# Writing out the last 26 instruction loops of an attention and expert layer

## The reference

```python
x = L0_attn_hidden_states                      # (1, 1024, 512)
xn = _layernorm(x, axis=-1)
x = x + _L0_attn_ref(xn, ...) + _L0_ffn_ref(xn, ...)

# attention: 32 heads, latent queries (rank 192) and keys/values (rank 64)
q_lat = rmsnorm(hidden_states @ q_a_w, q_a_norm_w)
q = (q_lat @ q_b_w)...                         # nope 128 + rope 64
ckv = hidden_states @ kv_a_w
scores = (q_nope . k_nope + q_pe . k_pe) * QKD ** (-0.5)
# indexer: 16 heads choose 128 keys for each query
iq = (hidden_states @ idx_wq_w)...; ik = hidden_states @ idx_wk_w
idx_scores = einsum(iw, relu(iq @ ik)) * IDX_D ** (-0.5)
_, topk_idx = jax.lax.top_k(where(causal, idx_scores, -inf), 128)
attn = softmax(where(topk_mask & causal, scores, -inf))
out = (attn @ v) @ o_w

# experts: 8 of rank 16, two for each row
w = gates of the top 2 of softmax(flat @ router_w.T + router_b)
out = einsum('ner,eor->no', (flat @ A) * w, Bm) * SCALING
```

## Time and profile before

| | us |
|---|---|
| median of 3 runs (lowest, highest) | 998.99 (997.48, 999.64) |
| profiled execution, its own time | 999.31 |
| its span, first to last instruction | 997.5 |
| busy: TensorE / VectorE / ScalarE / GpSimd | 895.8 / 740.7 / 680.4 / 449.0 |
| mean granted TensorE clock, share of full | 0.959 |

### The profile page before, as it was taken

How to read it: one execution, slowest core, us unless ns; L and a number is a source line. 1 busy time by engine, 2 the same in 40 slices (tenths; PEclk the granted TensorE clock), 3 DMA queues, 4 the chain that set the end, 5 groups by cost and what they waited for, 6 DMA issues and landing times.

```text
span 997.5 us, 23426 instructions
## 1 busy us (share of the span) xinstructions
PE 895.8 (90%) x7912; PEld 552.9 (55%) x7912; DVE 740.7 (74%) x1593; ACT 680.4 (68%) x1512; POOL 449.0 (45%) x307
## 2 busy tenths in 40 slices
PE   5979999977774689999999999999999999999998
PEld 2434554434441146666676666676766666675443
DVE  5386689999999968777887877787788778783000
ACT  3565779987873367887888788788778878872000
POOL 2194229875656643634554364446335544600000
PEclk9999999997767689999999999999999999999999
DMA  7012111112342920000000000000000000310211
GB/s 228 22 32 63 45 51 54 53 37 75 92 140 100 331 112 2 23 23 24 1 23 23 2 23 23 22 2 23 23 23 3 23 23 1 136 58 22 64 42 42
DMA packets 47261, 52.54 MB, mean 53 GB/s; under 512 B 5440, under 2 KB 31424, under 8 KB 47168
## 3 DMA queue, kind: packets, MB, share of 16 engines
q1 hardware_dynamic: 47168, 51.31, 15.8%
HBM read 36.62 MB, written 6.29 MB: 43 GB/s over the span
## 4 chain that ended last, share of the span: by engine, by line
PE 53%; issue 5%; DVE 4%; ACT 3%; DVEq 0%
PE psS L575 17%; PE psT L652 11%; PE psO L633 8%; PE psS L684 8%; ACT arena L714 2%; DVE arena L1202 2%; PE psT L560 2%; DVE arena L968 2%; PE psT L556 2%; PE psT L558 1%; PE psT L559 1%; PE psT L557 1%; PE psT L641 1%; PE psS L689 1%; ACT arena L914 0%
## 5 line engine op out<-in xcount | busy, mean ns | idle before, releaser
L714 ACT ACTIVATE arena<-psT 128x512 f16<-128x512 f32 (+5 forms) x544 | 262.9, 519 | 121.7 <-PE psT L652 79.3
L968 DVE SCALAR_TENSOR_TENSOR arena<-psT,arena 128x512 f16<-128x512 f32 (+3 forms) x392 | 205.6, 552 | 71.4 <-ACT arena L714 71.4
L575 PE MATMUL psS<-keyT,arena 128*128 128x512 f16 (+3 forms) x1152 | 230.6, 327 | 12.6 <-issue 11.7
L1202 DVE CUSTOM_DVE_ANT_0 arena<-psS,bias 128x1024 f32<-128x1024 f32 (+7 forms) x256 | 192.5, 752 | 53.5 <-PE psS L575 50.9
L914 ACT ACTIVATE arena<-arena,small 128x1024 f32<-128x1024 f32 (+7 forms) x256 | 199.1, 778 | 18.0 <-DVE small L1202 15.9
L652 PE MATMUL psT<-ident,arena 128*128 128x128 f32 x1152 | 176.9, 281 | 9.8 <-DVE arena L968 8.1
L633 PEld LDWEIGHTS psO<-val,arena 128*128 128x128 f16 x3456 | 132.1, 98 | 37.5 <-DVE arena L968 6.0
L575 PEld LDWEIGHTS psS<-keyT,arena 128*128 128x128 f16 x1152 | 103.8, 99 | 84.3 <-issue 30.9
L633 PE MATMUL psO<-val,arena 128*128 128x64 f16 x3456 | 142.7, 193 | 1.2 <-DVE arena L968 1.2
L652 PEld LDWEIGHTS psT<-ident,arena 128*128 128x128 f32 x1152 | 124.3, 142 | 13.3 <-issue 12.9
L1401 POOL TENSOR_TENSOR arena<-arena,cq 128x1024 f32<-128x1024 f32 x16 | 37.8, 2364 | 190.3 <-issue 181.2
(11 more groups left out here) (146 smaller groups left out, 1117.9 us busy)
## 6 DMA issues: line engine op xcount, KB each, us to landing
arena<-in_wiq SPq DMA_DIRECT2D x32, 256.0 KB, 2.8
arena<-in_ow SPq DMA_DIRECT2D x16, 512.0 KB, 4.9
arena<-arena SPq DMA_DIRECT2D x32, 256.0 KB, 2.4
arena<-in_qbT SPq DMA_DIRECT2D x16, 256.0 KB, 2.5
wvo_parts<-arena SPq DMA_DIRECT2D x16, 256.0 KB, 4.6
arena<-in_qpe SPq DMA_DIRECT2D x16, 128.0 KB, 2.8
arena<-in_x SPq DMA_DIRECT2D x8, 256.0 KB, 2.8
out<-arena SPq DMA_DIRECT2D x8, 256.0 KB, 2.0
```

The lines of the kernel that those rows point to most:

```text
L575: last = mm(psS[k % 2][:, c:c + w], Q[:, v, a, h, t * P:(t + 1) * P], keyT[:, b, h, c:c + w], start=(a, b) == (0, 0), stop=(a, b) == (1, 0))
L714: return nc.scalar.activation(dst, src, ACT.Copy, scale=scale)
L968: return v.scalar_tensor_tensor(out=dst, in0=src, scalar=scale, in1=hi, op0=ALU.mult, op1=ALU.subtract)
L1202: v.tensor_tensor_reduce(out=pr[:, k % 4, 0:kw], in0=psS[k % 2][:, 0:kw], in1=bias[:, TOFF[t]:TOFF[t + 1]], scale=-c_s, scalar=3e38, op0=A ...
```

## The change

All 26 loops are written out: each `with engine.Fori(a, b) as i:` becomes `for i in range(a, b):`, which the program that builds the kernel runs itself. The body is emitted once for every value of i with constants in the place of registers. Nothing else differs. One of each kind:

```diff
@@ SyncE, third stage
-            with sp.Fori(1, NP // 2) as i:
+            for i in range(1, NP // 2):
                 load_qw(2 * i, 0, False)
                 load_qw(2 * i + 1, 1, False)
@@ SyncE, value-output products
-            with sp.Fori(1, NP // OW_DEEP) as i:
+            for i in range(1, NP // OW_DEEP):
                 for u in range(OW_DEEP):
                     load_ow(OW_DEEP * i + u, u, False)
                     store_vo(OW_DEEP * i + (u - OW_DEEP), u)
@@ TensorE, projections, and the last stage
-            with pe.Fori(1, NT // 2 - 1) as i:
+            for i in range(1, NT // 2 - 1):
-            with pe.Fori(1, NT // 2) as i:
+            for i in range(1, NT // 2):
@@ ScalarE, third stage
-            with act.Fori(1, IH // 2) as i:
+            for i in range(1, IH // 2):
@@ VectorE, third and fourth stage
-            with dve.Fori(1, IH // 2) as i:
+            for i in range(1, IH // 2):
                 for u in range(2):
                     third(2 * i + u, u, False)
-            with dve.Fori(4, IH // 2) as i:
+            for i in range(4, IH // 2):
                 for u in range(2):
                     fourth(2 * i + u, u, False)
@@ GpSimd, third stage
-            with pool.Fori(1, IH // 2) as i:
+            for i in range(1, IH // 2):
                 for u in range(2):
                     third_sums(2 * i + u, False)
```

More of the change, by code:

```diff
@@ L518, in _ @@
             iq_head(IH, 0, 0, False)
-            with pe.Fori(0, IH // 2 - 1) as i:
+            for i in range(0, IH // 2 - 1):
                 for u in range(2):
@@ L751, in _ @@
             squares(0, True)
-            with act.Fori(1, NT // 2 - 1) as i:
+            for i in range(1, NT // 2 - 1):
                 for u in range(2):
@@ L842, in _ @@
             second_relu(1, 1, False)
-            with act.Fori(1, IH // 2 - 2) as i:
+            for i in range(1, IH // 2 - 2):
                 for u in range(2):
@@ L1131, in _ @@
             second(1, 1, False)
-            with dve.Fori(1, IH // 2 - 1) as i:
+            for i in range(1, IH // 2 - 1):
                 for u in range(2):
@@ L1277, in _ @@
             final(1, 1, True)
-            with dve.Fori(1, NT // 2) as i:
+            for i in range(1, NT // 2):
                 final(2 * i, 0, False)
@@ L1352, in _ @@
             gated_rows()
-            with pool.Fori(3, IH // 2 + 1) as i:
+            for i in range(3, IH // 2 + 1):
                 wq_parts(2 * i, 0)
@@ L1374, in _ @@
             second_sums(1, False)
-            with pool.Fori(1, IH // 2 - 2) as i:
+            for i in range(1, IH // 2 - 2):
                 for u in range(2):
@@ L1435, in _ @@
             rope_low(0, 0)
-            with pool.Fori(1, NP // OW_DEEP) as i:
+            for i in range(1, NP // OW_DEEP):
                 for u in range(OW_DEEP):
```

20 lines of the change are left out of this document (10 added, 10 removed).

## The result

| | before | after |
|---|---|---|
| median of 20 runs (lowest, highest), us | 998.60 (997.45, 1000.43) | 1000.74 (997.61, 1005.52) |
| profiled execution, its own time | 999.31 | 999.08 |
| its span | 997.5 | 997.1 |

A forecast was written before the change was run, and what follows sets the result against it. TensorE was taken to bound the first score and last stages, VectorE's top-128 search the stretch between 142 and 354 us. Terms -0.16, -0.2, -0.6 and -0.2 sum to -1.16 us: 998.99 to 997.8 us, range 994.0 to 1000.8.

The forecast's parts named there:

- Projection loop: Projections, 22 to 37 us: TensorE's idle time at the loop entry goes, -0.16 us.
- Latent products: GpSimd products before the first score loop: a VectorE shift may save or cost 0.95 us; taken as 0.
- Second and fourth stage: VectorE's top-k rounds: written-out and looped rounds already equal, 4.97 and 2.96 us, so 0.
- Third stage (a): Third score stage: fourteen loop rounds each 0.02 us longer than written-out ones; taken as -0.2 us.
- Third stage (b): Third score stage: GpSimd starting 0.2 to 0.4 us sooner shortens two collisions with VectorE, -0.6 us.
- new collisions: Rival, third stage: earlier GpSimd additions hold VectorE's small operations in five rounds, 1002.8 us; chance 0.12.
- Value-output products: Beside the fourth stage: SyncE issues loads and stores sooner, head pairs start earlier, -0.2 us.
- Head pairs: Sixteen head pairs, 354 to 905 us: already written out and untouched by the diff, 0.
- Last stage: Final stage: TensorE is full and the last handover to VectorE already short, 0.
- Instruction fetch: Rival: TensorE's longer program fetches five or six more code blocks, 1 us each, 1003.8 us; chance 0.04.
- branches: Rival: taken loop branches stall VectorE by at most 0.1 us in 17 rounds, removal gives 996.1 us; chance 0.02.
- Slower: Outcome for the whole kernel: measured time above 1001.0 us; chance 0.10, against 0.37 faster and 0.53 the same.

The follow-up runs named there:

- experiment 4: Against before: only ScalarE's and GpSimd's third-stage loops written out, 998.37 us; the whole change except the five third-stage loops, 998.87 us.
- only_third: Before with only the five loops of the third stage written out; 1000.46 us, ratio 1.0021.
- all_again: The whole change, unaltered, run and profiled once more against before; 999.97 us, ratio 1.0011.
- all_apart: Whole change plus the filler, VectorE's first two third-stage low parts reading PSUM instead of SBUF (results not the reference's); 998.15 us, ratio to before 0.9991.
- all_filled: The whole change plus the filler alone; 999.66 us, ratio to before 1.0009.
- all_gpsimd: Whole change plus the filler, two third-stage low parts per round moved from VectorE to GpSimd; 992.82 us, again 993.70, with parted loads 991.19.
- the filler: Eight unread TensorE matmuls added before its wait for the last third-stage low parts; alone on before 998.16 us, ratio 0.9987.
- third_filled: Before with the five third-stage loops written out and the filler added; 999.28 us, ratio 1.0000.
- before_apart: Before with the filler, VectorE's first two third-stage low parts reading PSUM instead of SBUF (results not the reference's); 999.01 us, ratio 0.9998.
- before_gpsimd_low: Before, loops kept, with the filler and two low parts of each third-stage round moved from VectorE to GpSimd; 995.37 us, ratio 0.9970.
- all_gpsimd_split: Whole change, filler, two third-stage low parts moved to GpSimd, rope columns' load under its own semaphore; 991.19 us, ratio to before 0.9929.

## Why the prediction was wrong, point by point

- *Projection loop, -0.16 us:* right, the idle time is gone.
- *Latent products, 0 with ends of -0.95 and +0.95:* right in the one trace, the long product changed places. What was missed is that the weight splits beside them can be held too, and that TensorE's pause behind one draws a lower clock: up to 1.9 us later at the third stage (experiment 4).
- *Second and fourth stage, 0:* right for the rounds, 4.97 and 2.96 us unchanged. But the fourth stage is more than its rounds, and the prediction had no term for its two casts and three masks, which GpSimd can hold as well: together they took 4.2 us in before, and 3.5 in after (2.60 + 0.90).
- *Third stage (a), -0.2 us:* too large, and harmless. Without the stretched time the 15 rounds are 69.13 us in before (71.49 - 2.36) and 69.01 in after (70.39 - 1.38), but 69.0 also in the other looped kernels. The 0.02 us a round were the last decimal.
- *Third stage (b), -0.6 us:* this step failed. In the one pair of profiles the sum of the stretched time did fall, from 2.9 to 1.8 us with round 15, further than the 2.4 that was named as the sign; and yet the kernel is slower over many runs. It took the collisions of one trace as fixed in place and shortened two of them by the lead that GpSimd gets. The lead is real. Eight kernels enter with GpSimd 0.7 us behind w1lo in round 0 and 0.2 us in round 1. In round 2 it is 1.16 to 1.57 us behind in the four of them with ScalarE's and GpSimd's loops, and 0.36 to 1.05 us in the four where these two are written out. But GpSimd drifts 0.5 us a round against VectorE, so that a lead changes which rounds are hit, and brings more of the expensive kind, where an addition begins just ahead. The mean went from 1.55 to 3.22 us in five profiles each, +1.7 us where the sum had -0.6. The rival "new collisions" had this mechanism, with the right place and the right point of decision (0.32 us), but a chance of 0.12 and one fixed price of 5 us. The price is a distribution: the profiles lie between 1.4 and 7.3 us of stretched time, where the loops have 0.7 to 2.4. The argument "most rounds have over 1 us of room" was read from one trace, of a phase that moves.
- *Value-output products, -0.2 us:* the sign in the one trace is right (358.52 against 359.18), the reason was not. SyncE's issue doesn't decide this start. The chain begins with 20 products on TensorE, whose time goes with the clock granted there (5.2 to 9.1 us in the profiles of this study). The prediction costed them at nothing and had no row for them. They are a part of it only: in after they ended at 310.09 us, 1.9 us later than in before, and the last store came 0.7 us sooner. From their end to that store it is 48.4 us in after, 51.0 in before and 50.8 in only_third; why, stays open. The products took 9.0 and 9.1 us in after and only_third, and 6.7 to 7.7 us in the eight other kernels without the filler; whether written-out loops draw the low level more often, or these two did by chance, stays open.
- *Head pairs, 0:* almost. Two of the periods are 34.67 us instead of 34.53, the same two in after, all_again, all_apart and all_filled, 0.3 us in all. The cause stays open.
- *Last stage, 0:* right.
- *Instruction fetch, branches:* the first did not show, with six more blocks and the same 11.7 us of "issue"; the second neither, with the rounds unchanged.
- *"Slower" above 0.2%, 0.10, against 0.37 for faster:* the profile before already had 2.4 us of collisions whose place would be drawn anew. A redraw can go up as easily as down, which the chances did not respect.

Some 0.2 us lie outside the span: the difference between time and span is 1.8 us in before and 2.0 to 2.2 in most runs of the change, all_filled and all_apart, but 1.8 in the all_gpsimd kernels. That is a tenth of the loss, and unexplained.

## What to carry to other kernels

Before costing an edit that only shifts engines against each other, list the operations that can hold one another (here VectorE's with two SBUF inputs, its masks and casts, and GpSimd's), and compare the pace of the two engines. If the paces differ, the phase drifts, the collisions seen in one trace are one draw, and the expected gain of a shift is not their size; remove one of the two partners instead, here two operations of 0.29 us each: with the filler 0.3% with the loops, and 0.7% with the loops written out and the loads parted. The loops cost nothing here on the engine that always has work: its rounds were equal to 0.02 us. Whether they cost something on a chain that others wait for isn't shown. Judge by many runs, since a single profile of the slower kernel was here faster than that of the faster one.

## What the runs showed of the hardware

- A VectorE operation of 0.29 us with two SBUF inputs took up to 1.4 us beside GpSimd's additions (third_filled); with one input in PSUM it was never stretched, in 3 x 64 operations, also where GpSimd's additions started 0.15 us ahead of it. The step from the search to it is 0.13 us a round longer then.
- VectorE operations with one input, in SBUF, were held as well: three masks took 0.90 us in after and 3.67 in third_filled, and a cast of 64x1024 took 0.67 us in before and 1.53 in only_third.
- The same 20 matmuls took 5.2, 6.8 or 9.1 us, with the granted clock at 1.00, at 0.5 and then 1.00, and at 0.5, behind a stage in which TensorE works in bursts. Eight useless matmuls in its wait of 3.6 us before them made the kernel 1.3 us faster (ratio 0.9987), and its runs half as wide. In before_apart, before_gpsimd_low and all_gpsimd_split the 20 products took 6.8, 6.8 and 7.6 us in spite of them.
- On GpSimd the 128x128 and 64x128 subtractions take 0.43 us each, with 0.33 us from the last one to the next addition, where a wait stands between them.
